# Sums of a graph attention stage with the gathered rows as stationary operand, and one load moved behind its loop

## The chip, the cores and the metric

The kernel runs on one core of one Trainium2 chip. The metric is the device time of one execution in microseconds (us); the median of three runs counts. A core has five engines that run side by side and meet through semaphores: TensorE (PE; its weight loads are PEld), VectorE (DVE), ScalarE (ACT), GpSimd (POOL) and SyncE (SP), which issues transfers. PSUM, the memory that TensorE writes, has 8 banks. An instruction that waits for a semaphore holds everything behind it on its engine.

## The reference

Four graph layers stand behind each other over 3125 nodes with 128 features and 103125 edges sorted by destination. Each adds its result to `x`. The third is the graph attention layer (GAT) with 2 heads:

```python
xl = (h @ Wl + bl).reshape(n, H, D)        # H = 2, D = 128
xr = (h @ Wr + br).reshape(n, H, D)
e = leaky_relu(xl[src] + xr[dst], 0.2)
alpha = einsum('ehd,hd->eh', e, att)
alpha = segment_softmax(alpha, dst, n)
out = segment_sum(xl[src] * alpha[..., None], dst, n).mean(axis=1)
return residual + out + h @ res_W + bias
```

The first layer is a graph convolution, the second an additive attention with 4 heads of 32 channels (same frame of a kernel stage as the third, with one bank more for each step), the fourth an interaction layer.

## The kernel before

The edges are cut into 202 tiles of 512 (4 sub-tiles of 128). The destinations of a tile lie in a window of 20 nodes. `attend` is called twice: for the second layer and, with `gat` true, for the third, in the span from about 2060 to 3360 us. What follows is the third layer's.

Each engine runs `over_tiles`: in step s it does its list of pieces, each for the tile s minus the piece's lag, and the order of the list is the order on the engine. The steps of a ring of 8 tiles make one loop body.

- POOL gathers for a tile the rows of its 512 source nodes (1 KB each) by four indirect DMAs (line 897) into one of 8 slots `rows(t)`. Before that it waits until `sums_ready` says that the tile 8 before has been summed.
- SP loads, for two tiles at once, the windows and the local places of the edges (lines 1457, 1462).
- PE in step s: `scores` of tile s-3 (lines 2101, 2106), `features` of s-1 (turns the gathered rows, line 2088, and adds the window's rows, line 2092), `turn_sums` of s-6 (line 2152), `turn_top` of s-4 (line 2128), `turn` of s-4 (the weights, line 2119), `sums` of s-5 (line 2140).
- ACT: `raise_scores` of s-3 (the exponential, line 2178), `activate` of s-1 (line 2170), `copy_sums` of s-5 (line 2184).
- DVE: `tops` of s-3 (lines 2228, 2230, 2235), `onehots` of s (line 1477), `keep_sums` of s-6 (line 2260), `leaky` of s-1 (line 2221), `best_of_nodes` of s-4 (lines 2253, 2256), `edge_weights` of s-4 (line 2246).

The sums of a tile: the stationary operand is the weights of one sub-tile and one head, 128 edges x 32 cells, the moving operand the gathered rows, 128 edges x 128 features. The result, 64 cells x 128 features for both heads, lies in bank 6. ACT copies it to `tile_rows`, PE turns it to features x cells in bank 7, DVE copies 20 of 32 cells of each head to `partial`. A product of float32 is two instructions in the records, so the 8 products of a tile are 16 records.

In `sum_counted`, a stage of the first convolution (from 452 to 600 us), the counts of one group of 24 tiles are loaded in three parts while the counts of the last tile are made again in a loop of `k.rebuild` rounds; `k.rebuild` is a number that the kernel computes, 1 for these inputs. PE waits for each part with a count that is made of it (line 1420).

## Time and profile before

| | |
|---|---|
| median of 3 runs | 4912.31 us (4910.18 to 4916.3) |
| span of the profiled execution | 4898.1 us |
| PE busy, share of the span | 3999.0 us, 82% |
| PEld | 2260.3 us, 46% |
| DVE | 2847.4 us, 58% |
| ACT | 1737.4 us, 35% |
| POOL | 2828.1 us, 58% |
| line 897, gathers of both attention stages, 1616 | about 947 ns each |
| line 2140, sums of the third layer, 3232 records | 202 x 16 |
| line 2184, copies, 202 | 252 / 258 / 262 ns (lowest, median, highest) |
| line 2152, turns, 202 | 217 / 243 / 338 ns |
| line 2260, DVE's copies, 202 | 176 / 198 / 201 ns |

The runs' times are some 14 us over the span of the records, which leaves out start and end. How to read the rows below: a row of a timeline has start, length, engine, line, operation, out<-in, shapes and in brackets the engine's idle time before it with what ended it (records of one kind are merged, xN); a row of groups has busy time, mean ns, idle time before and who ended it; a row of stretches has the length, then busy time and records of PE, PEld, DVE, ACT and POOL, PE's granted clock (1.00 is full), the share of the DMA engines and GB/s; a row of waits has the total, the number and the longest. Starts of TensorE's records can be trusted more than their ends. "issue" is waiting for nothing that the records show. Releasers are inferred: the latest event is named, which may not be the cause.

### The profile page before, as it was taken

What the parts mean: (1) busy time and instruction counts of PE and PEld (TensorE: products, weight loads), DVE (VectorE), ACT (ScalarE), POOL (GpSimd) and SP (SyncE); (2) the same over time, 40 slices, a digit from 0 to 9 for tenths busy, and PEclk for the clock granted to TensorE, in tenths of its full rate; (3) what the DMA queues carried; (4) which work ended last, traced back from release to release, by engine and by line L of the source; (5) the groups of instructions that cost most, each with busy time, mean ns of one, the idle gap of its engine ahead of it and who ended that gap; (6) DMA issues with size and microseconds to landing.
All of it is one profiled execution on the core that took longest, in us unless ns stands there. A gap on an engine that the chain in (4) does not pass through costs nothing. (4 is left out here: it accounts for less than half of the span.)

```text
span 4898.1 us, 89702 instructions
## 1 busy us (share of the span) xinstructions
PE 3999.0 (82%) x22566; PEld 2260.3 (46%) x22566; DVE 2847.4 (58%) x8457; ACT 1737.4 (35%) x4474; POOL 2828.1 (58%) x3060
## 2 busy tenths in 40 slices
PE   3997927788887877488888888885399999999987
PEld 1344414445544544344444444442256655556652
DVE  7994032333333334555555555556678888888868
ACT  3773023344344334333333333331322222222227
POOL 0122356666666663555555555554368888888862
PEclk8998957776777777688988888886699999999999
DMA  2333422222222221333333333330056666666650
GB/s 80 91 87 103 147 71 57 57 56 57 57 56 57 56 57 27 113 98 96 97 97 96 96 97 96 97 96 18 21 97 104 105 105 104 104 105 104 104 110 13
DMA packets 377425, 402.41 MB, mean 82 GB/s; under 512 B 86457, under 2 KB 322502, under 8 KB 377030
## 3 DMA queue, kind: packets, MB, share of 16 engines
q0 software_dynamic: 151904, 198.72, 21.0%
q1 hardware_dynamic: 225382, 202.21, 14.4%
q8 instruction: 43, 0.70, 0.1%
q14 instruction: 96, 0.79, 0.1%
HBM read 312.91 MB, written 87.78 MB: 82 GB/s over the span
## 5 line engine op out<-in xcount | busy, mean ns | idle before, releaser
L897 POOL DMA_INDIRECT gathered<-table,sources x952 | 903.6, 949 | 600.6 <-issue 259.9
L1709 POOL DMA_INDIRECT sums<-gathered,idx x606 | 988.7, 1632 | 217.8 <-issue 166.4
L1571 PE MATMUL bank<-wide 128*128 128x512 bf16 x3636 | 851.5, 379 | 0.0
L2228 DVE TENSOR_REDUCE neg_raw<-bank 80x1 f32<-80x512 f32 (+1 forms) x404 | 276.6, 685 | 725.9 <-remote 252.1
L897 POOL DMA_INDIRECT wide<-table,sources x464 | 438.7, 946 | 275.1 <-issue 125.7
L1571 PEld LDWEIGHTS bank<-wide 128*128 128x128 bf16 x3636 | 347.7, 98 | 364.1 <-issue 1.7
L2178 ACT ACTIVATE msg<-bank,neg_top 80x512 f32<-80x512 f32 (+1 forms) x404 | 275.7, 682 | 643.1 <-DVE neg_top L2230 353.6
L1222 POOL TENSOR_TENSOR acc<-acc,msg 128x20 f32 x404 | 108.3, 268 | 411.2 <-issue 244.6
L2221 DVE TENSOR_TENSOR zact<-zact,bank 128x512 f32<-128x512 f32 x404 | 259.5, 683 | 123.1 <-ACT zact L2170 72.9
L2106 PE MATMUL bank<-zact,att_cells 128*32 128x512 f32 x808 | 289.4, 732 | 37.9 <-issue 36.2
L2088 PEld LDWEIGHTS bank<-ident,gathered 128*128 128x128 f32 x1360 | 191.8, 165 | 258.0 <-issue 232.2
L2109 PE MATMUL bank<-zact,att_cells 128*80 128x512 f32 x404 | 301.6, 838 | 6.6 <-issue 6.6
L2246 DVE COPY edge_rows<-bank 128x320 f32<-128x320 f32 (+1 forms) x404 | 183.2, 453 | 203.5 <-remote 132.7
L2144 PE MATMUL bank<-edge_rows,gathered 128*128 128x80 f32 x1088 | 193.9, 337 | 92.5 <-DVE edge_rows L2246 81.9
L2088 PE MATMUL bank<-ident,gathered 128*128 128x128 f32 x1360 | 237.4, 317 | 35.4 <-issue 26.4
L2119 PE MATMUL bank<-ident,msg 80*128 80x80 f32 (+1 forms) x1616 | 215.5, 262 | 61.5 <-issue 33.9
L897 POOL DMA_INDIRECT h_nm<-table,sources x200 | 189.4, 947 | 130.5 <-DMA wide<-table,sources 69.3
L2190 ACT COPY partial<-bank 32x20 f32 (+1 forms) x808 | 132.6, 164 | 357.5 <-remote 239.5
L1169 DVE TENSOR_SCALAR gathered<-iota_c,partial 128x500 f16<-128x500 f16 x808 | 257.6, 339 | 1.7 <-issue 1.3
L2170 ACT ACTIVATE zact<-bank 128x512 f32<-128x512 f32 x404 | 216.8, 588 | 98.1 <-DMA window<-parts 81.2
L1178 PE MATMUL bank<-gathered,zact 128*128 128x500 f16 x812 | 209.3, 381 | 49.4 <-ACT zact L1285 28.1
L1622 ACT COPY gathered<-bank 128x437 f32<-128x437 f32 x202 | 106.1, 525 | 337.0 <-PE bank L1597 249.7
(406 smaller groups left out, 7603.9 us busy)
## 6 DMA issues: line engine op xcount, KB each, us to landing
zact<-in_src_flat SPq DMA_DIRECT2D x202, 192.0 KB
edge_rows<-in_attr_rows SPq DMA_DIRECT2D x202, 128.0 KB
dst_pair<-local_rows SPq DMA_DIRECT2D x177, 128.0 KB
gathered<-table,sources POOLq DMA_INDIRECT x952
dst_pair<-local_rows SPq DMA_DIRECT2D x202, 64.0 KB
counts<-wide SPq DMA_DIRECT2D x4, 3000.0 KB
counts<-fm_ab SPq DMA_DIRECT2D x4, 3000.0 KB
fm_ab<-counts SPq DMA_DIRECT2D x4, 3000.0 KB, 11.0
```

The costliest lines, as they stand in the source:

```text
L897: pool.indirect_dma_start(out=g[:, j, :], out_offset=None, in_=table, in_offset=bass.IndirectOffsetOnAxis(ap=mine, axis=0)).then_inc(rows_ ...
L1169: hot = dve.tensor_scalar(k.cell_hot[slot][:, j, :], k.iota_c[:, :], own, None, ALU.is_equal)
L1571: pe.matmul(k.bank[b][:, :], k.split[t.two][:, c, :], k.source_hot[t.two][:, b * CHUNK:(b + 1) * CHUNK], start=first, stop=c == PARTS - 1, ...
L1709: pool.indirect_dma_start(out=k.sums[j], out_offset=bass.IndirectOffsetOnAxis(ap=k.idx[t.slot][:, j:j + 1], axis=0), in_=out_rows(t)[:, j, ...
L2088: pe.matmul(z_bank(t, h)[:, j * P:(j + 1) * P], g[:, j, h * F:(h + 1) * F], k.ident[:, :], is_transpose=True, start=(j == 0), stop=False, ...
L2106: mm = pe.matmul(score_bank(t)[own_cells(h), :], a.att[h][:, own_cells(h)], k.zact[t.two][:, h, :], start=False, stop=True, skip_group_che ...
L2109: mm = pe.matmul(score_bank(t), a.att[0][:, :], k.zact[t.two][:, 0, :], start=False, stop=True)
L2119: mm = pe.transpose(weight_bank(t)[:, j * cells:(j + 1) * cells], raised(t)[:, j * P:(j + 1) * P], k.ident[lanes(t), lanes(t)])
L2170: act.mul(k.zact[t.two][:, h, :], z_bank(t, h)[:, :], 0.2).then_inc(slope_ready, 1)
L2178: act.activation(raised(t), score_bank(t), ACT.Exp, bias=k.neg_top[lanes(t), bass.ds(t.t, 1)], accum_out=k.weight_sum[lanes(t), bass.ds(t. ...
L2221: m = dve.tensor_tensor(za, za, z_bank(t, h)[:, :], ALU.max)
L2228: dve.tensor_reduce(raw, score_bank(t), AX.X, ALU.max, negate=True).then_inc(top_found, 1)
```

## The change

In the third layer the operands of the sums change places: the gathered rows of a sub-tile and a head (128 x 128) are stationary, and the weights (128 edges x 32 cells) move. The result is features x cells at once, 128 x 64 in bank 7. ACT's `copy_sums` and PE's `turn_sums` go, with their semaphores; DVE's `keep_sums` reads the sums themselves and waits for `sums_ready`. PE's `sums` of a tile now wait until DVE has kept those of the tile before, for the bank is one. The second layer's sums are as they were.

In `sum_counted` two parts of three are loaded in the loop, and the third once behind it, before SP's count that lets PE begin; the waits of PE are for constants.

```diff
+            second_there, rounds_done = st.sem("second_there"), st.sem("rounds_done")
...
-                    for landed in begun:
+                    for landed in begun[0:2]:
                         sp.sem_inc(landed, 16)
+
+                    def load_third(i):
+                        lo, hi = thirds[i]
+                        sp.dma_start(k.counts[0][:, lo:hi, :], k.all_counts[lo:hi, :, :].rearrange(
+                            "t p c -> p t c")).then_inc(begun[i], 16)
                     with sp.Fori(0, k.rebuild) as n:
-                        for (lo, hi), landed in zip(thirds, begun):
-                            sp.wait_ge(landed, n * 16 + 16)
-                            sp.dma_start(k.counts[0][:, lo:hi, :], k.all_counts[lo:hi, :, :].rearrange(
-                                "t p c -> p t c")).then_inc(landed, 16)
+                        for i in range(2):
+                            sp.wait_ge(begun[i], n * 16 + 16)
+                            load_third(i)
...
                         sp.sem_inc(free, 1)
+                        sp.wait_ge(begun[1], n * 16 + 32)
+                        sp.sem_inc(rounds_done, 1)
+                    sp.sem_inc(second_there, 1)
+                    load_third(2)
...
                         cell_counts(k, pe, 0, k.bank[0]).then_inc(counted, 1)
+                        pe.wait_ge(begun[0], n * 16 + 32)
...
-                            if first(now):
-                                pe.wait_ge(begun[i], k.rebuild * 16 + 16)
+                            if first(now) and i == 1:
+                                pe.wait_ge(second_there, 1)
+                            if first(now) and i == 2:
+                                pe.wait_ge(begun[2], 16)
...
-        return k.bank[6][0:cells, 0:F] if gat else k.bank[6 + t.two][:, 0:cells]
-
-    def turned_bank(t):
-        return k.bank[7][:, 0:cells]
+        return k.bank[7 if gat else 6 + t.two][:, 0:cells]
...
-                    wait_count(pe, copied if gat else kept, t.t if gat else t.t - 1)
+                    wait_count(pe, kept, t.t if gat else t.t - 1)
...
-                        for j in range(SUB):
-                            for h in range(heads):
-                                mm = pe.matmul(sum_bank(t)[own_cells(h), :], weights(t)[:, j, own_cells(h)],
-                                               g[:, j, h * F:(h + 1) * F], start=(j == 0), stop=(j == SUB - 1))
+                        for h in range(heads):
+                            for j in range(SUB):
+                                mm = pe.matmul(sum_bank(t)[:, own_cells(h)], g[:, j, h * F:(h + 1) * F],
+                                               weights(t)[:, j, own_cells(h)], start=(h == 0 and j == 0),
+                                               stop=(h == heads - 1 and j == SUB - 1), skip_group_check=True)
...
-                def turn_sums(t):
-                    pe.wait_ge(copied, t.t + 1)
-                    wait_count(pe, kept, t.t)
-                    pe.sem_inc(turns_begun, 1)
-                    pe.transpose(turned_bank(t), k.tile_rows[t.two][:, :],
-                                 k.ident[0:cells, 0:cells]).then_inc(sums_turned, 1)
                 if gat:
-                    over_tiles(pe, k.tiles, [(3, scores), (1, features), (6, turn_sums), (4, turn_top), (4, turn),
+                    over_tiles(pe, k.tiles, [(3, scores), (1, features), (4, turn_top), (4, turn),
                                              (5, sums)], ring=ring)
...
-                def copy_sums(t):
-                    act.wait_ge(sums_ready, t.t + 1)
-                    wait_count(act, sums_turned, t.t - 1)
-                    act.copy(k.tile_rows[t.two][:, :], sum_bank(t)).then_inc(copied, 1)
...
-                    over_tiles(act, k.tiles, [(3, raise_scores), (1, activate), (5, copy_sums)], ring=ring)
+                    over_tiles(act, k.tiles, [(3, raise_scores), (1, activate)], ring=ring)
...
                 def keep_sums(t):
-                    dve.wait_ge(sums_turned, t.t + 1)
+                    dve.wait_ge(sums_ready, t.t + 1)
                     dve.tensor_copy(a.partial[:, :, bass.ds(t.t, 1), :].rearrange("p z t n -> p z (t n)"),
-                                    turned_bank(t).rearrange(
+                                    sum_bank(t).rearrange(
                                         "p (z c) -> p z c", z=heads)[:, :, 0:WIN]).then_inc(kept, 1)
```

On TensorE, one step of the third layer's loop reads like this before (a row's shape is the result's; a float32 product counts once here and is two records in the trace):

```order
L2092 MATMUL bank<-onehot_t,window 128x512 x2
L2152 MATMUL bank<-ident,tile_rows 128x64
L2128 MATMUL bank<-top_cells,own 2x20
L2119 MATMUL bank<-ident,msg 128x64 x4
L2140 MATMUL bank<-gathered,edge_rows 32x128 x8
L2101 MATMUL bank<-h_nm,far 64x512
```

and like this with the change (the lines are those of the changed kernel, 8 higher here):

```order
L2100 MATMUL bank<-onehot_t,window 128x512 x2
L2136 MATMUL bank<-top_cells,own 2x20
L2127 MATMUL bank<-ident,msg 128x64 x4
L2148 MATMUL bank<-edge_rows,gathered 128x32 x8
L2109 MATMUL bank<-h_nm,far 64x512
```

The turn of the sums is gone, and the sums stand where they stood, with the operands in the other roles. On VectorE the order stays: the copy out of the bank (`partial<-bank`, line 2258 of the changed kernel) stands behind the score maximum, its two followers and the one-hot of its step, and PE's sums of the same step now wait for it:

```order
L2226 TENSOR_REDUCE neg_raw<-bank 64x1
L2228 ISA
L2228 TENSOR_SCALAR neg_top<-neg_raw 64x1
L2233 TENSOR_SCALAR top_cells<-place,neg_top 64x20
L1489 TENSOR_SCALAR h_nm<-dst_pair,iota_w,always 128x512
L2258 REGISTER_ALU
L2258 COPY partial<-bank 128x2x20
```

On SyncE, in the counts stage, three loads stood in the loop ahead of the store of the last tile's counts:

```order
L1375 DMA wide<-counts 128x8x500 x3
L1377 REGISTER_ALU
L1378 ISA
L1378 DMA counts<-fm_ab 128x500
L1372 REGISTER_ALU
L1372 COMPARE_AND_BRANCH
L1390 DMA fm_ab<-counts 128x24x500
```

With the change the third stands behind the loop, ahead of the next group's load:

```order
L1376 DMA wide<-counts 128x8x500 x2
L1382 REGISTER_ALU
L1383 ISA
L1383 DMA counts<-fm_ab 128x500
L1387 REGISTER_ALU
L1378 REGISTER_ALU
L1378 COMPARE_AND_BRANCH
L1376 DMA wide<-counts 128x8x500
L1399 DMA fm_ab<-counts 128x24x500
```

The third load has moved past the store and its landing.

## Rows read from the trace of the kernel before

**Rows 1.** Groups of instructions by shape, 2400 to 3200 us.

```profile
L897 POOL DMA_INDIRECT gathered<-table,sources x249 | 235.4, 945 | 166.4 <-DMA wide<-table,sources 97.0 <-issue 59.5 <-PE bank L2140 9.9
...
L2228 DVE TENSOR_REDUCE neg_raw<-bank 64x1 f32<-64x512 f32 x124 | 85.1, 687 | 180.4 <-DMA dst_pair<-local_rows 153.4 <-PE bank L2106 21.2 <-issue 5.0
```

**Rows 2.** Busy time by stretches: the third layer's stage, the second's.

```profile
2200.00:2700.00 500.00, 424.65 (x2957) 221.66 (x2957) 282.29 (x775) 157.85 (x386) 294.69 (x312) 0.88 0.34 97
900.00:1300.00 400.00, 334.30 (x1406) 201.95 (x1405) 132.09 (x427) 166.40 (x504) 250.64 (x264) 0.72 0.22 56
```

**Rows 3.** Timeline of all engines, one tile's period, 2711 to 2719 us.

```profile
2711.19 0.26 ACT L2184 COPY tile_rows<-bank 64x128 f32<-64x128 f32 x1 [1.42 <-DMA wide<-table,sources]
...
2711.94 0.95 POOL L897 DMA_INDIRECT gathered<-table,sources  x1 [1.91 <-DMA wide<-table,sources]
...
2712.56 1.07 PE L2140 MATMUL bank<-gathered,edge_rows 128*32 128x128 f32 x16
2712.66 0.68 ACT L2178 ACTIVATE msg<-bank,neg_top 64x512 f32<-64x512 f32 x1 [1.21 <-PE bank L2119]
...
2713.36 0.20 DVE L2260 COPY partial<-bank 128x40 f32 x1
...
2715.70 0.94 POOL L897 DMA_INDIRECT gathered<-table,sources  x1 [0.30 <-issue]
...
2715.90 0.60 PE L2092 MATMUL bank<-onehot_t,window 60*128 60x512 bf16 x2
2717.73 0.68 DVE L2228 TENSOR_REDUCE neg_raw<-bank 64x1 f32<-64x512 f32 x1 [1.45 <-DMA dst_pair<-local_rows]
2717.74 0.26 ACT L2184 COPY tile_rows<-bank 64x128 f32<-64x128 f32 x1 [3.20 <-DMA wide<-table,sources]
...
2718.14 0.29 PE L2152 MATMUL bank<-ident,tile_rows 64*128 64x64 f32 x1 [1.64 <-ACT tile_rows L2184]
...
2718.41 0.94 POOL L897 DMA_INDIRECT gathered<-table,sources  x1 [1.77 <-DMA wide<-table,sources]
```

**Rows 4.** Waits, 2400 to 3200 us.

```profile
ACT tile_rows L2184 <- DMA wide<-table,sources: 264.4, 92, 5.8
DVE neg_raw L2228 <- DMA dst_pair<-local_rows: 153.4, 67, 4.8
...
PE bank L2152 <- ACT tile_rows L2184: 70.5, 59, 4.2
```

**Rows 5.** Timeline of TensorE, a step at full clock without waits.

```profile
2739.07 0.40 PE L2101 MATMUL bank<-onehot_t,far 64*64 64x512 bf16 x1
...
2741.85 0.22 PE L2152 MATMUL bank<-ident,tile_rows 64*128 64x64 f32 x1
...
2742.13 0.46 PE L2119 MATMUL bank<-ident,msg 64*128 64x64 f32 x4
2742.52 1.07 PE L2140 MATMUL bank<-gathered,edge_rows 128*32 128x128 f32 x16
2743.51 0.40 PE L2101 MATMUL bank<-h_nm,far 64*64 64x512 bf16 x1
```

**Rows 6.** Timeline of TensorE in the second layer: full-width float32 loads.

```profile
1312.15 1.06 PE L2144 MATMUL bank<-edge_rows,gathered 128*128 128x80 f32 x8
1313.14 0.41 PE L2101 MATMUL bank<-zact,far 64*80 64x512 bf16 x1
```

**Rows 7.** Timeline of TensorE: the sums at the half clock.

```profile
2719.18 1.92 PE L2140 MATMUL bank<-wide,edge_rows 128*32 128x128 f32 x16
```

**Rows 8.** Timeline of all engines, start of the sums of counts.

```profile
465.17 0.45 PE L1195 MATMUL bank<-wide,h_nm 128*128 128x160 f16 x2 [6.74 <-SPq L1387]
```

**Rows 9.** The next groups' loads of counts, line 1390.

```profile
L1390 SPq DMA_DIRECT2D wide<-counts x4: 372/376/393, 483.0 to 575.7; - x4
```

**Rows 10.** DMA issues, 440 to 500 us: size and median time to landing.

```profile
wide<-counts SPq DMA_DIRECT2D x3, 1000.0 KB, 7.7
```

**Rows 11.** Groups of instructions by shape, second layer, 900 to 1800 us.

```profile
L2228 DVE TENSOR_REDUCE neg_raw<-bank 80x1 f32<-80x512 f32 x148 | 101.0, 683 | 304.3 <-remote 177.7 <-PE bank L2109 81.0 <-issue 45.6
```

More of the change, by code:

```diff
@@ L2049, in attend @@
         sums_ready, kept = st.sem("sums_ready"), st.sem("kept")
-        copied, sums_turned = st.sem("copied"), st.sem("sums_turned")
         cells_ready, top_turned, top_kept, best = (st.sem("cells_ready"), st.sem("top_turned"),
```

## The prediction

> **What bounds the kernel now.** I first read the groups of instructions and the busy time of the stage that the change touches, for its pace and its limits; then its waits; then one tile's timeline. The attention stage of the third layer (202 tiles, from about 2060 to 3360 us) is some 27% of the span. In 800 us of its middle 124 tiles pass (L2228 runs once a tile) [rows 1], so a tile takes 6.45 us and the stage 202 x 6.45 = 1303 us. No engine fills this: TensorE is busy 85% at a granted clock of 0.88, POOL 59%, VectorE 56%, ScalarE 32% [rows 2].
>
> POOL does more than its busy share says. It issues four gathers a tile, 0.945 us each, one every 1.25 us [rows 1, 3]; four in a row are 3 x 1.25 + 0.95 = 4.70 us, and endless ones would give 5.0 us a tile. The rest is a gap between two tiles: 2715.70 + 0.94 = 2716.64 to 2718.41, 1.77 us (0.30 would be the usual one). POOL waits there for `sums_ready`, since the sums of a tile free the slot of the next gather.
>
> The strange thing is when `sums_ready` comes. The 16 sum records of L2140 end at 2713.63, and the array goes on with L2101, L2106, L2088 and L2092 until 2716.50. But all that wait for TensorE's results resume together at 2717.7: ScalarE's copy L2184 (it waits for the sums) at 2717.74, VectorE's L2228 (for the scores) at 2717.73, POOL at 2718.41 [rows 3]. The step before is alike: the copy at 2711.19, POOL at 2711.94. So a result that the records have ended at 2713.6 is seen 4 us later, about 1 us after the last gather of the burst has ended. The views put this to "DMA" as the latest event: 264 us of ScalarE's and 153 us of VectorE's waits in 800 us [rows 4]. Of the 166.4 us that POOL idles before its 249 gathers of one name, 97.0 are put to DMA, 59.5 are the usual issue gaps, and only 9.9 are put to L2140 itself [rows 1]. I read it so: while POOL issues a burst, TensorE's signals are held, and a tile costs burst plus release plus restart, 4.70 + about 1.05 + 0.75 = 6.5 us. The cause of the hold the trace doesn't show.
>
> **The change part by part, in the attention stage.**
> *Copy and turn removed.* ScalarE loses L2184, 0.26 us a tile; it is not the limit, worth 0. TensorE loses L2152: in a tight step it and L2128 take 2742.13 - 2741.85 = 0.28 us of the array [rows 5], half of it 0.14. It also loses the wait before it (70.5 us in 59 cases of 124, 0.57 us a tile [rows 4]), but that wait is for a release that comes from the burst, so what follows is not earlier by it.
> *The sums turned round.* Before, 16 records load 32 columns each, and two heads run side by side: L2140 takes 2743.51 - 2742.52 = 0.99 us [rows 5]. After, 16 records load 128 columns and stream 32. The nearest rows are the second layer's sums, the same load of 128 x 128 f32: 8 records in 1313.14 - 1312.15 = 0.99 us [rows 6], 0.124 us each. 16 make 1.98 us, +0.99. The lowest bound is the pace of the four L2119 in the same stage, (2742.52 - 2742.13) / 4 = 0.098, which gives 1.56 us, +0.57; a gain is excluded, since a record takes 0.99 / 16 = 0.062 us now, less than either. I take +0.9, nearer to the second layer's form. A tight step is now 2743.51 - 2739.07 = 4.44 us [rows 5]; after, 4.44 - 0.14 + 0.9 = 5.2 us (4.87 to 5.29).
>
> The trace has 0.124 us for a 128-column load of 80 streamed columns, and 0.062 us a record for the 32-column loads. The Trainium skill (TensorE: Matmul & The Clock Gate, section LDWEIGHTS) says that a load's time goes with the columns loaded, P / 1.2 ns, 107 ns for 128 whatever is streamed; this would make the sums 1.71 us and the step about 5.0. It also says (TensorEngine Tiling (Array Packing), section When to Use Tiling) that with a free dimension of 64 or less one should swap the operands and tile the columns, which is what the kernel does before and the change undoes. By that rule the change makes TensorE slower, and the rows agree.
>
> *A new wait.* `sum_bank` is one bank and VectorE empties it itself, so TensorE's sums of tile s-5 wait for VectorE's keep_sums of s-6. That stands behind the score maximum, its two followers and the one-hot in VectorE's step: the release at 2711.2 (ScalarE's copy), L2260 from 2713.36 to 2713.56 [rows 3], thus 2.3 us after the release. Before, the sums began 2712.56, 1.4 us after it. Now they begin at 2.3, end at 2.3 + 1.9 = 4.2; behind them are queued scores (1.3), features (1.5) and the two turns (0.5), to 7.5 us, 1.0 us into the next period of 6.5. Who waits? POOL needs the sums by its next release at 6.5: 2.3 us of room. VectorE needs the scores (5.5) at 6.5: 1.0 of room. ScalarE's activation needs the features (7.0 = 0.5 into the next period), but it stands behind the exponential, which starts 1.5 after the release (2712.66): room again. So at the full clock all is hidden, and the period stays with POOL's burst: 0 us a tile.
>
> *At the half clock* the step is not covered so well: the 16 records of L2140 last 1.92 instead of 1.07 us [rows 5, 7], and a whole step at it is up to 2 x 5.2 = 10.4 against 2 x 4.44 = 8.9 us, +1.5. The mean of 0.88 says that a quarter of the time is at 1.2 GHz (0.24 x 1300 = 312 us, 30 to 35 steps). It falls after idle stretches of TensorE (that of 1.64 us before 2718.14, behind which the slow L2140 stands [rows 3, 7]); the new step keeps TensorE busy 0.8 us longer, so there should be fewer. I take +0.1 us of each 1.5, as the ring of 8 slots and the 1 us of room a tile take up the rest: 33 x 0.1 = 3 us.
>
> *Head and tail of the stage:* the last copy and turn go (0.26 + 0.24), the longer sums come (0.9), about +0.4 us.
>
> **The counts.** The last third of the first group's load is now issued once, behind the loop. Before, TensorE starts its sums at 465.17, when SyncE has passed `stored` [rows 8]. Now SyncE issues the third before it lets TensorE go (the increment of `loaded[0]` is behind it): an issue takes 0.37 us on L1390 [rows 9], and I take +0.5 with what stands around it, 1.5 at most. It lands about 7.7 us later [rows 10], near 474; TensorE comes to it after two thirds of the group. The next load but one, L1390 at 483.0 [rows 9], is released by the group's end, so the group lasts 17.8 us and the third is needed at 477.4. Hidden by 3 us. The next group's load of 3000 KB stands behind these 1000 KB and may come some us later than now; nothing waits for it before 483. A wait put where none was costs 0.
>
> **Sum:** 4898.1 + 3 + 0.4 + 0.5 = 4902 us of span. The median is 14.2 us over that span (4912.3), which lies outside the records and stays: 4916.2 us.
>
> **The rivals.**
> *Slower: TensorE becomes the bound.* Its step of 5.2 us at a clock of 0.88 is 5.9 us, against 6.45: only 8% of room. If every half-clock step costs its full 1.5 us: 33 x 1.5 = 50 us, 4966. If the clock fell to the second layer's 0.72 [rows 2], 5.2 / 0.72 = 7.2 us a tile, +0.77 x 202 = 156 us, 5070. It decides from the point where the step over the clock exceeds 6.45, a clock of 0.81. For it: the second layer has just this form of sums, and the lower clock. Against: the clock falls here behind idle stretches, and TensorE will have shorter ones.
> *Faster: the hold comes with the column-tiled sums.* In the step shown it begins at L2140, while the turn just ahead of it (L2119) is seen at once: ScalarE's L2178 goes on at 2712.66 [rows 3]. If full-width sums are seen when they end, at 4.2 us, POOL would not wait: 5.2 us a tile by TensorE, -1.2 x 202 = -240 us, 4670. If it only loosens to the pace of the second layer (148 tiles in 900 us [rows 11], 6.08 us), -0.37 x 202 = -75 us, 4840. Against: the second layer's sums are full-width already, and VectorE waits 177.7 us there for something that is put to no instruction [rows 11].
> *The change does nothing that lasts:* that is my forecast.
>
> **How the numbers follow.** A measurement of this kernel can tell about 0.2%, 10 us. Chances: hidden (4903 to 4922) 0.38; slower, 4922 to 4990, 0.25, and over 4990, 0.08; faster, 4840 to 4903, 0.20, and under 4840, 0.09. The range 4840 to 4990 leaves 0.17 out; the likeliest case alone is 4903 to 4922. Both signs are open, so: faster 0.29, same 0.38, slower 0.33.
>
> **What would show it.** Right: tiles still 6.45 us apart, POOL's gap still 1.8 us, the new L2148 16 records in 1.6 to 2.0 us, started by VectorE's L2258, ScalarE waiting before its exponential instead of its copy. Wrong: POOL's gaps near 0.3 us (the hold was the column tiling's), or POOL's waits put to L2148 in dozens and a clock under 0.85 (TensorE bounds). In the counts, a wait of TensorE at 477 us would show the third late.

## The result: 2% slower

| | before | changed |
|---|---|---|
| median | 4911.25 us (4 runs, 4898.11 to 4916.3) | 5009.3 us (4 runs, 5008.49 to 5011.22) |
| profiled execution, span | 4898.1 us | 5009.5 us |
| third layer, first to last of 202 tiles | 1278.0 us, 6.36 us a tile | 1372.8 us, 6.83 us a tile |
| TensorE busy, granted clock, 2200 to 2700 us | 85%, 0.88 | 100%, 0.75 |

The ratio is 1.020, 95% interval 1.019 to 1.022. The prediction was 4916 us with a range of 4840 to 4990: wrong, 93 us too low and outside its range. The two profiled executions differ by 111.4 us. Of these 94.8 lie in the attention stage of the third layer; it starts 6.9 us later (2075.2 instead of 2068.3), and 9.7 us come behind it. The last two amounts lie in code that the change does not touch, but for the counts, which became faster (below); repetitions of the kernel before differ among themselves by 18 us.

### The profile page after: what moved, and what is told of

Read it like the earlier page. It is cut to its first block and busy times, and to the rows that moved or that the text cites. A ratio compares the mean times of both kernels' runs of the same rounds, so it can differ in the third digit from the quotient of the medians.

```text
span 5009.5 us, 88649 instructions
## 1 busy us (share of the span) xinstructions
PE 4265.8 (85%) x22364; PEld 2490.1 (50%) x22364; DVE 2855.1 (57%) x8457; ACT 1700.7 (34%) x4272; POOL 2897.4 (58%) x3060
## 5 line engine op out<-in xcount | busy, mean ns | idle before, releaser
L2226 DVE TENSOR_REDUCE neg_raw<-bank 80x1 f32<-80x512 f32 (+1 forms) x404 | 277.1, 686 | 849.9 <-PE bank L2114 416.6
L2114 PE MATMUL bank<-zact,att_cells 128*32 128x512 f32 x808 | 376.5, 1031 | 15.8 <-issue 15.8
L1222 POOL TENSOR_TENSOR acc<-acc,msg 128x20 f32 x404 | 172.8, 428 | 350.0 <-issue 188.4
L2096 PEld LDWEIGHTS bank<-ident,gathered 128*128 128x128 f32 x1360 | 215.6, 183 | 307.2 <-issue 286.2
L2096 PE MATMUL bank<-ident,gathered 128*128 128x128 f32 x1360 | 258.6, 339 | 28.0 <-DMA window<-parts 16.2
L1169 DVE TENSOR_SCALAR gathered<-iota_c,partial 128x500 f16<-128x500 f16 x808 | 277.2, 373 | 7.7 <-PE bank L1178 5.9
L2153 PEld LDWEIGHTS bank<-edge_rows,gathered 128*128 128x128 f32 x1088 | 172.1, 241 | 113.1 <-DVE edge_rows L2244 75.7
```

The source lines that it names most:

```text
L1169: hot = dve.tensor_scalar(k.cell_hot[slot][:, j, :], k.iota_c[:, :], own, None, ALU.is_equal)
L2096: pe.matmul(z_bank(t, h)[:, j * P:(j + 1) * P], g[:, j, h * F:(h + 1) * F], k.ident[:, :], is_transpose=True, start=(j == 0), stop=False, ...
L2114: mm = pe.matmul(score_bank(t)[own_cells(h), :], a.att[h][:, own_cells(h)], k.zact[t.two][:, h, :], start=False, stop=True, skip_group_che ...
L2153: mm = pe.matmul(sum_bank(t), g[:, j, :], weights(t)[:, j, :], start=(j == 0), stop=(j == SUB - 1))
L2226: dve.tensor_reduce(raw, score_bank(t), AX.X, ALU.max, negate=True).then_inc(top_found, 1)
```

## The profile after

Busy time by stretches of the changed kernel; the columns are those of [rows 2]: stretch, length, busy time of PE, PEld, DVE, ACT and POOL, TensorE's granted clock, DMA share, GB/s. The first line is the whole stage, the second answers to the first line of [rows 2], the last is the second layer.

```profile
2060.00:3470.00 1410.00, 1382.55 (x7441) 813.56 (x7442) 744.02 (x2041) 374.58 (x808) 749.03 (x809) 0.74 0.30 87
2200.00:2700.00 500.00, 498.85 (x2718) 291.78 (x2716) 269.50 (x732) 136.54 (x294) 277.75 (x293) 0.75 0.32 91
...
900.00:1300.00 400.00, 325.17 (x1391) 195.63 (x1391) 131.88 (x427) 165.06 (x501) 250.55 (x264) 0.74 0.21 56
```

TensorE has no idle time left, 498.85 of 500 us, and at the same time its clock is lower: 0.75 where [rows 2] have 0.88. The second layer is as before.

Groups and waits of the changed kernel, 2400 to 3200 us (busy time and mean of one, idle time ahead and what ended it; then engine, waiting line, releaser, us, times, longest). They answer to [rows 1] and [rows 4]; L2226 is the old L2228.

```profile
L897 POOL DMA_INDIRECT gathered<-table,sources x233 | 220.8, 948 | 176.2 <-PE bank L2148 121.2 <-issue 53.1 <-DMA wide<-table,sources 1.9
...
L2226 DVE TENSOR_REDUCE neg_raw<-bank 64x1 f32<-64x512 f32 x117 | 80.6, 689 | 242.6 <-PE bank L2114 240.4 <-issue 2.2
```

```profile
ACT msg L2181 <- DVE neg_top L2228: 329.1, 68, 5.6
...
DVE neg_raw L2226 <- PE bank L2114: 240.4, 116, 2.8
...
POOL gathered L897 <- PE bank L2148: 121.2, 58, 4.1
```

117 tiles pass in 800 us where it was 124. "DMA" as the releaser has all but gone, 1.9 us where [rows 1] have 97.0: POOL now waits for the sums' own records (L2148), VectorE for the scores' (L2114). The engines wait for TensorE, and it is late because it is busy.

One period of TensorE in the changed kernel, then POOL's gathers around it (start, length, engine, line, operation, count, in brackets the idle time ahead):

```profile
2739.14 0.20 PE L2136 MATMUL bank<-top_cells,own 64*2 64x20 f32 x2
...
2739.27 0.46 PE L2127 MATMUL bank<-ident,msg 64*128 64x64 f32 x4
...
2739.66 1.97 PE L2148 MATMUL bank<-edge_rows,h_nm 128*128 128x32 f32 x16
...
2741.57 0.63 PE L2109 MATMUL bank<-onehot_t,far 64*64 64x512 bf16 x1
...
2742.13 1.92 PE L2114 MATMUL bank<-zact,att_cells 128*32 128x512 f32 x4
...
2743.98 1.53 PE L2096 MATMUL bank<-ident,wide 128*128 128x128 f32 x8
...
2745.45 0.60 PE L2100 MATMUL bank<-onehot_t,window 60*128 60x512 bf16 x2
```

```profile
2739.33 0.95 POOL L897 DMA_INDIRECT h_nm<-table,sources  x1 [0.30 <-issue]
2742.42 0.95 POOL L897 DMA_INDIRECT h_nm<-table,sources  x1 [2.14 <-PE bank L2148]
```

The 16 records of the sums take 2741.57 - 2739.66 = 1.91 us. Directly behind them the clock is at its lower level, 1.2 GHz: one bf16 record takes 0.63 instead of 0.40 us, the four of L2114 1.92 instead of 1.05. During L2096 it is back at 2.4 GHz, stays there to the end of the sums, and falls again. Taken in short stretches, the granted clock is 1.00 from 2738.2 to 2741.4 us and 0.50 from 2741.6 to 2744.8, and so on with each tile: about half of the time at either level. The next tile's L2148 begins at 2746.50, 6.84 us after this one, and many tiles in a row repeat this to one or two hundredths of a microsecond. Where the clock stays up for a step, the step is shorter:

```profile
2700.75 0.40 PE L2109 MATMUL bank<-onehot_t,far 64*64 64x512 bf16 x1
2701.08 1.05 PE L2114 MATMUL bank<-zact,att_cells 128*32 128x512 f32 x4
...
2704.17 1.96 PE L2148 MATMUL bank<-edge_rows,gathered 128*128 128x32 f32 x16
2706.05 0.40 PE L2109 MATMUL bank<-onehot_t,far 64*64 64x512 bf16 x1
```

That is 2706.05 - 2700.75 = 5.30 us, of which the sums are 1.88 and nothing is idle. The other 1.54 us of the 6.84 are the lower clock.

## The experiments

The labels' first letters are groups. The kernels of a group ran on one chip, beside the kernel before on the same chip, and the chips turned out to be of two kinds. (Each was used in one group only, so it is not shown that the chip makes the difference and not its state at the time.) On one kind before takes 4907 to 4935 us, as in the result; on the other 4381 to 4388 us. The same unchanged code of the second layer takes 6.1 to 6.2 us a tile on the first and 5.01 to 5.04 on the second. The traces tell why. On the first kind what TensorE has finished becomes visible late, as described with [rows 3]; on the second the waiting engines go on within tenths of a microsecond. I call them the late and the prompt chips. Only ratios within one group are compared.

| kernel | chip | median, us | before there | ratio (95%) | third layer, us a tile | clock in it |
|---|---|---|---|---|---|---|
| f1_counts | late | 4903.85 | 4907.42 | 0.999 (0.998 to 1.000) | 6.38 | 0.88 |
| f2_grouped | late | 4905.97 | 4907.42 | 1.000 (0.999 to 1.001) | 6.39 | 0.93 |
| f3_bank7 | late | 4962.72 | 4907.42 | 1.012 (1.010 to 1.014) | 6.60 | 0.86 |
| f4_half | late | 4903.73 | 4907.42 | 1.000 (0.998 to 1.002) | 6.35 | 0.80 |
| h1_after (the change) | late | 5016.48 | 4935.08 | 1.016 (1.014 to 1.018) | 6.86 | 0.75 |
| h2_wide | late | 5029.93 | 4935.08 | 1.020 (1.017 to 1.022) | 6.79 | 0.83 |
| h3_counts | late | 4933.93 | 4935.08 | 1.000 (0.999 to 1.001) | 6.45 | 0.88 |
| h4_early | late | 4936.66 | 4935.08 | 1.000 (0.999 to 1.001) | 6.43 | 0.82 |
| j1_counts | late | 4936.44 | 4933.26 | 1.000 (0.999 to 1.001) | 6.46 | 0.86 |
| j2_keepfirst | late | 4993.14 | 4933.26 | 1.012 (1.010 to 1.013) | 6.69 | 0.87 |
| i2_after (the change) | prompt | 4739.68 | 4387.97 | 1.080 (1.079 to 1.082) | 6.76 | 0.76 |
| i3_wide | prompt | 4490.06 | 4387.97 | 1.024 (1.022 to 1.026) | 5.50 | 0.99 |
| i1_keepfirst | prompt | 4451.05 | 4387.97 | 1.014 (1.013 to 1.016) | 5.35 | 1.00 |
| i4_pause | prompt | 4737.79 | 4387.97 | 1.080 (1.078 to 1.081) | 6.77 | 0.90 |
| g1_wide | prompt | 4493.26 | 4381.49 | 1.024 (1.022 to 1.027) | 5.55 | 0.98 |
| g2_split | prompt | 5730.28 | 4381.49 | 1.308 (1.306 to 1.310) | 11.65 | 0.50 |
| g3_pause | prompt | 4740.19 | 4381.49 | 1.082 (1.080 to 1.084) | 6.78 | 0.89 |
| g4_pausewide | prompt | 4754.16 | 4381.49 | 1.084 (1.081 to 1.086) | 6.79 | 0.89 |

The microseconds a tile are the time from the first to the last start of VectorE's reduction of the scores, over 201. The clock is that of 800 us in the middle of the stage, for g2_split of 500 us.

### Which part of the change costs

f1_counts has the change's `sum_counted` and the old `attend`.

> Only the part of the change in the counts: the register wait is mended, the sums stay as before (column-tiled, copied and turned). Both theories expect the slowdown to be that of the sums, so this kernel stays within 0.2% of before, with the counts part 2 to 3 us shorter (9.6 instead of 12.1 us from first load to first sum), and the readers of TensorE's results in the third layer again 3 to 4 us late from the start of the gathers on. If instead the slowdown of 98 us came with the counts, this kernel would be at 5009 us.

The time is that of before, and it was so twice more (h3_counts, j1_counts). The three medians differ from before's by -3.6, -1.2 and +3.2 us, all within the noise. The counts are worth nothing that can be measured in the kernel's time; their stretch did become shorter. SyncE's issues of the kernel before, then of f1_counts, and TensorE's first sum in it:

```profile
453.07 2.60 SPq L1375 DMA_DIRECT2D wide<-counts  x3
459.32 0.37 SPq L1378 DMA_DIRECT2D counts<-fm_ab  x1
```

```profile
453.17 1.02 SPq L1376 DMA_DIRECT2D wide<-counts  x2
459.46 0.37 SPq L1383 DMA_DIRECT2D counts<-fm_ab  x1
462.07 0.37 SPq L1376 DMA_DIRECT2D wide<-counts  x1
```

```profile
462.55 0.45 PE L1195 MATMUL bank<-wide,h_nm 128*128 128x160 f16 x2 [3.96 <-SPq L1396]
```

From the first load to the first sum 462.55 - 453.17 = 9.38 us, where before had 465.17 [rows 8] - 453.07 = 12.10. The store (`counts<-fm_ab`) is what TensorE's start hangs on; with two loads ahead of it instead of three it is done 2.6 us after its issue (462.07), before it took until about 465.1. The transfers' own account agrees: from issue to landing the store takes 2.2 us in f1_counts and 5.5 us before.

So the loss is that of the sums: what the counts add to it is under the noise.

### Is it TensorE's work?

f4_half leaves half of the products of the sums out (and with them half of the result):

```diff
-                            for j in range(SUB):
+                            for j in range(SUB // 2):
```

> The changed kernel with half of the products of its sums left out (8 records a tile instead of 16), so that a part of the result is not computed. If TensorE's time is what now bounds the third layer, each tile gets at least 0.95 us shorter: 4820 us or less, down to 4640 us where GpSimd at 5.0 us a tile takes over. If waits between the engines set the 6.84 us a tile, the time stays at 5009 us.

With 8 records less a tile, 0.95 us, all of the 98 us come back: 4903.73 beside 4907.42. But no more than that, so neither of the two times expected came (4820 us or less, or 5009). The tile takes 6.35 us as before, not 5.0. And the signals are late again, with the very form of products under which they looked prompt:

```profile
2656.15 0.96 POOL L897 DMA_INDIRECT gathered<-table,sources  x1 [0.30 <-issue]
2656.16 0.65 PE L2100 MATMUL bank<-h_nm 60*128 60x512 bf16 x2
...
2657.27 1.08 PE L2148 MATMUL bank<-edge_rows,gathered 128*128 128x32 f32 x8
2657.41 0.95 POOL L897 DMA_INDIRECT gathered<-table,sources  x1 [0.30 <-issue]
...
2660.05 1.09 ACT L2173 ACTIVATE zact<-bank 128x512 f32<-128x512 f32 x2 [3.67 <-DMA window<-parts]
...
2660.99 0.95 POOL L897 DMA_INDIRECT gathered<-table,sources  x1 [2.63 <-DMA wide<-table,sources]
```

L2100 ends at 2656.81 and L2148 at 2658.28. ScalarE, which waits for L2100, goes on only at 2660.05, and POOL, which waits for L2148, at 2660.99. POOL's last gather ended at 2658.36; the release comes 1.69 us behind it (1.1 in [rows 3]). So, as I read it, there are two limits that lie close together on this chip: the old one (a burst of gathers plus the late release, 6.4 us a tile) and TensorE's step, 6.84 us with its clock down. The change went from the first to the second.

### Were the late signals a matter of the column-tiled sums?

Both kernels keep the old sums with the counts of the change. f2_grouped puts all products of head 0 ahead of those of head 1, so that neighbours no longer lie on different columns of the array. f3_bank7 puts the sums into bank 7, turns them there too, and waits for VectorE as the change does:

```diff
 # f2_grouped
-                        for j in range(SUB):
-                            for h in range(heads):
+                        for h in range(heads):
+                            for j in range(SUB):
 # f3_bank7
-        return k.bank[6][0:cells, 0:F] if gat else k.bank[6 + t.two][:, 0:cells]
+        return k.bank[7][0:cells, 0:F] if gat else k.bank[6 + t.two][:, 0:cells]
-        return k.bank[7][:, 0:cells]
+        return k.bank[7][:, F:F + cells]
-                    wait_count(pe, copied if gat else kept, t.t if gat else t.t - 1)
+                    wait_count(pe, kept, t.t if gat else t.t - 1)
```

> The counts of the change, and the sums column-tiled as before, but with all products of one head before those of the other, so that no two neighbours lie on different columns of the array. Theory A (late signals come from products of two column groups that run interleaved): signals are prompt, the 16 products take 1.6 to 2.0 us, and the time is 4700 to 4850 us. Theory B (column tiling or the small stationary operand as such makes the signals late): still 3 to 4 us late, 4910 us and, if the sums take longer without their neighbour, up to 0.5 us a tile more. Theory C (the bank or the waits around the sums): still late, 4910 us.

> The counts of the change, and the column-tiled sums of before, but in bank 7 and with the wait that the changed kernel has in front of its sums. Theory C (what the change took away is a matter of the bank or of where the sums wait): signals are prompt and the time is 4700 to 4850 us. Theories A and B (the form of the products): signals still 3 to 4 us late, the new wait is hidden, 4900 to 4925 us.

In both the signals stay late (ScalarE's copy of the sums waits 223.0 us in 71 cases for "DMA" in 800 us of f3_bank7, 267.1 us in 91 cases in f1_counts), so theories A and C fall, and f4_half took B away. The form of the sums does not make the signals late. Grouped, the 16 records take 1.53 instead of 1.07 us (without a neighbour on the other columns), and this costs nothing that can be measured. Turned round they take 1.97 by the same rows, so about half of what the change adds to the sums comes already with the loss of the side-by-side products.

f3_bank7 missed its expectation in a way that matters: 59 us more than f1_counts. A wait of this kind, which the prediction called hidden, is not. TensorE's wait in 800 us of f3_bank7:

```profile
PE bank L2152 <- DVE partial L2272: 132.0, 75, 6.1
```

The wait for VectorE's copy holds TensorE 132 us in 75 cases. In the changed kernel the wait at this place is 3.1 us, since TensorE there comes to it late anyway. The two are not quite the same wait: in f3_bank7 VectorE's copy must itself wait for ScalarE's copy and TensorE's turn, which the changed kernel no longer has, so 59 us is more than the changed kernel's wait need cost. The keepfirst kernels below price that one.

### What brings the clock down?

g1_wide, h2_wide and i3_wide are one kernel: the changed one, with each product streaming the weights of both heads, 64 columns instead of 32. The half that is of the other head is never read.

```diff
-        return k.bank[7 if gat else 6 + t.two][:, 0:cells]
+        return k.bank[7][:, 0:3 * cells] if gat else k.bank[6 + t.two][:, 0:cells]
...
-                                mm = pe.matmul(sum_bank(t)[:, own_cells(h)], g[:, j, h * F:(h + 1) * F],
-                                               weights(t)[:, j, own_cells(h)], start=(h == 0 and j == 0),
+                                mm = pe.matmul(sum_bank(t)[:, h * cells:(h + 1) * cells], g[:, j, h * F:(h + 1) * F],
+                                               weights(t)[:, j, :], start=(h == 0 and j == 0),
```

> The changed kernel, but each product of the sums streams the weights of both heads (64 columns instead of 32) and the half that is of the other head is not read. At full clock a product is bound by its load of 128 columns (118 ns a record), so the sums still take about 1.9 us. Theory P (the clock falls because so few columns are streamed in the stretch of the sums): the granted clock in the third layer rises from 0.74 to 0.85 or more, TensorE's step falls under 6.45 us a tile, and the limit of before takes over again (GpSimd's burst of four gathers, signals of TensorE held until about 1 us behind it): 6.4 to 6.5 us a tile, 4890 to 4925 us. Theory Q (the clock falls because TensorE has no idle time): clock stays near 0.74 and the time at 4990 to 5030 us, up to 5080 us if the wider products take longer.

The clock is that of theory P, 0.98. Neither theory's time can be judged, because g1_wide ran on a prompt chip, where the changed kernel had not run. i2_after and i3_wide put both on one chip, again a prompt one.

> The changed kernel as the anchor of this call. Where signals are late (before at 4905 to 4935 us): 5009 to 5016 us. Where they are prompt (before at 4381 us): by theory P (few streamed columns let the clock fall, whatever the signals do) 6.84 us a tile here too and 4760 to 4800 us, over 200 us above the wide kernel's 4493 us; by theory R (the clock falls only together with late signals) 4480 to 4500 us like the wide one.

> The wide kernel (64 streamed columns) beside it. Where signals are late: 5015 to 5040 us, clock 0.83 in the third layer. Where prompt: 4493 us, clock 0.98, 5.5 us a tile.

Stretches of 800 us of i2_after, then of i3_wide, then of i1_keepfirst (i3_wide with another order on VectorE, described below):

```profile
2000.00:2800.00 800.00, 799.58 (x4379) 471.03 (x4378) 434.78 (x1184) 219.07 (x473) 447.40 (x473) 0.76 0.32 92
```

```profile
2000.00:2800.00 800.00, 791.13 (x5409) 513.57 (x5410) 533.76 (x1461) 263.07 (x584) 552.47 (x586) 0.99 0.39 113
```

```profile
2000.00:2800.00 800.00, 800.00 (x5564) 523.61 (x5565) 544.19 (x1505) 269.51 (x601) 568.20 (x602) 1.00 0.40 117
```

TensorE idles 0.4, 8.9 and 0.0 us in them. With 32 streamed columns its clock is 0.76, with 64 it is 0.99 and 1.00, and i3_wide is 250 us faster than i2_after although it streams twice the columns. The third row leaves no room for theory Q: busy all of the 800 us, TensorE keeps its full clock. A step of the wide one on the prompt chip:

```profile
2403.62 0.40 PE L2109 MATMUL bank<-h_nm,far 64*64 64x512 bf16 x1
2403.95 1.05 PE L2114 MATMUL bank<-zact,att_cells 128*32 128x512 f32 x4
2404.94 1.09 PE L2096 MATMUL bank<-ident,wide 128*128 128x128 f32 x8
...
2407.26 1.97 PE L2148 MATMUL bank<-edge_rows,gathered 128*128 128x64 f32 x16 [0.18 <-DVE partial L2258]
2409.16 0.40 PE L2109 MATMUL bank<-onehot_t,far 64*64 64x512 bf16 x1
```

The wide sums take 2409.16 - 2407.26 = 1.90 us, as the narrow ones: at this size the weight load sets the pace, and the doubled columns are free. So the clock does not fall here because TensorE is idle, and not because it is busy. It falls behind the 1.9 us in which TensorE loads weights and streams 32 columns a product, and stays up behind the same 1.9 us with 64 (theory P); that the number of streamed columns makes the difference is shown by this one edit, how the chip weighs them is not. The Trainium skill (TensorE: Matmul & The Clock Gate, section HAM oscillation) gives as its rule to leave no long idle gaps on TensorE; i2_after has none, 0.42 us of idle time in 800 us, and runs at 0.76.

g2_split was to tell a long stretch of such products from the mean of the period: the products of head 0 moved to behind the scores.

```diff
-                    over_tiles(pe, k.tiles, [(3, scores), (1, features), (4, turn_top), (4, turn),
-                                             (5, sums)], ring=ring)
+                    over_tiles(pe, k.tiles, [(3, scores), (5, first_sums), (1, features), (4, turn_top), (4, turn),
+                                             (5, sums)], ring=ring)
```

> The changed kernel, with the products of head 0 moved to behind the scores, so that the 16 products of a tile stand in two stretches of 8 with the tile's transposes of the gathered rows between them; same work. Theory P1 (a long stretch of products with few columns makes the clock fall): clock up to 0.85 or more, 4890 to 4930 us. Theory P2 (what counts is the work of the whole period, not where it stands): clock about 0.74, 5000 to 5020 us.

Neither came: 5730 us. The first products now wait right behind the scores until VectorE has emptied the bank of the tile before, and that copy stands in VectorE's step behind the reduction of those scores:

```profile
PE bank L2144 <- DVE partial L2267: 145.5, 68, 2.3
```

That is 2.1 us in each of 68 tiles of 800 us, and the clock is at 0.50 through the whole stage, with TensorE busy 82%. It says that the lower level can last for 2.3 ms; since a wait was added with the split, it does not decide between P1 and P2.

### And on the late chip?

> The changed kernel once more, on the same chip as the other three of this call, as their anchor. On a chip where TensorE's signals come late while GpSimd issues (before at 4907 us): 5009 us again, granted clock 0.74 in the third layer and 6.84 us a tile. On a chip where they come promptly (before at 4381 us, as in the call with the wide and the paused kernels): slower than before as well, by more than the 112 us of the wide kernel if the clock falls here too (6.84 us a tile, 4760 to 4800 us), by 80 to 112 us if it does not.

> The changed kernel with 64 instead of 32 streamed columns in each product of its sums, again. Where signals are late: theory P (few streamed columns let the clock fall) has the clock back at 0.85 or more, and TensorE no longer bounds the tile, so that the 6.4 to 6.5 us of before return, 4890 to 4930 us. Theory Q (being busy without a break lets the clock fall) has it at 0.74 and 5000 us or more. Where signals are prompt: 4493 us again, 5.5 us a tile, and by theory P over 200 us less than the changed kernel, by theory Q the same as it.

> The sums of before with the counts of the change, as the picture of the kernel before on this chip: within 0.2% of before on either. Where before takes 4907 us the signals of TensorE come 3 us late from the start of the gathers on; where it takes 4381 us they are prompt, a tile of the third layer takes about 5.0 us, and GpSimd's burst of four gathers (4.7 us) is what bounds it.

Here the clock rises as well, 0.75 to 0.83, and it gives nothing: 5029.93 beside 5016.48. So theory P has nearly its clock and misses its time by 100 us. Where the clock is up, TensorE's step of 5.3 us is under the old limit, and POOL's gathers show the old picture. h2_wide:

```profile
2705.79 1.39 PE L2148 MATMUL bank<-edge_rows,gathered 128*128 128x64 f32 x11
...
2707.11 0.40 PE L2109 MATMUL bank<-onehot_t,far 64*64 64x512 bf16 x1
...
2707.53 0.95 POOL L897 DMA_INDIRECT gathered<-table,sources  x1 [0.30 <-issue]
...
2710.34 0.94 POOL L897 DMA_INDIRECT gathered<-table,sources  x1 [1.87 <-DMA wide<-table,sources]
```

The sums end at 2707.11, inside the burst; POOL resumes at 2710.34, 1.86 us after its last gather's end, and the wait is put to DMA again. In the changed kernel the sums end at 2741.57, and POOL's last gather had ended at 2740.28: TensorE is so late that nothing is left to hold. I take this to be why the signals looked prompt there.

Why, then, does h2_wide lose 95 us? Half of POOL's bursts in it start 6.3 to 6.7 us apart, but in the whole stage 18 pairs, the stage's first left aside, are 8 to 9.7 us apart. The kernel before, f1_counts and h3_counts have no such pair. In all 18 TensorE is at its lower clock for half of the time or more. Here are three rows of TensorE and one of POOL in such a period, and then its stretch in the columns of [rows 2]:

```profile
2158.40 0.63 PE L2109 MATMUL bank<-onehot_t,far 64*64 64x512 bf16 x1
2164.45 3.67 PE L2148 MATMUL bank<-edge_rows,gathered 128*128 128x64 f32 x16
2168.06 0.63 PE L2109 MATMUL bank<-onehot_t,far 64*64 64x512 bf16 x1
2168.92 0.95 POOL L897 DMA_INDIRECT gathered<-table,sources  x1 [4.95 <-PE bank L2148]
```

```profile
2159.26:2168.92 9.66, 9.66 (x39) 6.08 (x37) 4.58 (x14) 1.86 (x4) 3.79 (x5) 0.50 0.24 73
```

A step of TensorE at the lower clock takes 2168.06 - 2158.40 = 9.66 us without a pause, 3.61 of them the sums, and POOL waits for it. On a late chip the turned sums therefore cost by the steps that fall into the lower clock, even where the mean clock is most of the way back.

j2_keepfirst and i1_keepfirst take the wait for the bank out of the wide kernel, by putting VectorE's copy at the head of its step:

```diff
-                    over_tiles(dve, k.tiles, [(3, tops), (0, onehots), (6, keep_sums), (1, leaky),
+                    over_tiles(dve, k.tiles, [(6, keep_sums), (3, tops), (0, onehots), (1, leaky),
```

> The wide kernel, with VectorE's copy of the sums put at the head of its step, ahead of the reductions and the one-hot rows, so that bank 7 is free sooner. If the wait for the bank is what is left where the clock stays up (21 to 48 us of TensorE's idle time in 800 us of the wide kernel), 20 to 50 us less than the wide kernel; if TensorE's step and the late signals bound it, the same within 0.3%.

> The wide kernel with VectorE's copy of the sums at the head of its step, again. Where signals are prompt: 4451 us (a TensorE step of 5.3 us against GpSimd's 5.0 us a tile), 60 us above before. Where signals are late: if the wait for bank 7 is what keeps the wide kernel at 5030 us, 4950 to 5000 us; if the late signals do, 5010 us or more.

39 us less than the wide kernel on the prompt chip (4451.05 for 4490.06). On the late ones the loss against before went from 94.9 to 59.9 us, 35 us less. It is the best kernel with the whole of the sums turned round, and still slower than before on both: on the prompt chip its tiles are 5.32 us apart, each a full TensorE step without a break. Before is 63 us faster there, which over 202 tiles is 0.31 us a tile less, an estimate of 5.0 us: the pace of POOL's four gathers at one every 1.25 us. The 60 us that remain on a late chip can be followed in the traces of j2_keepfirst and j1_counts. I sort the distances between the starts of POOL's bursts, from the tenth tile on, by the mean clock granted in them. At 0.95 or more they are alike, 6.29 us (110 of 192) and 6.33 us (95). At 0.60 or less they are 8.04 us (27) and 6.53 us (17). 27 x (8.04 - 6.29) = 47 us less 17 x (6.53 - 6.33) = 3 us makes an estimate of 44 us, and the two profiled executions differ by 42.8. What remains is thus the steps at the lower clock again. The mean clock of the stage doesn't show it, 0.87 in j2_keepfirst and 0.86 in j1_counts. In j1_counts the time at the lower clock comes in 62 stretches, 6 of them over 8 us, in j2_keepfirst in 33, 17 of them over 8 us, up to 24, so that whole steps fall into it. With the wait for the bank in place, in h2_wide, the distances at 0.95 or more are 6.51 us (82) against 6.32 in h3_counts (96): 0.19 us a tile, 38 us in 202, is what this wait costs at the full clock.

h4_early moves the old sums 0.6 us forward, ahead of the turns of the weights:

```diff
-                    over_tiles(pe, k.tiles, [(3, scores), (1, features), (6, turn_sums), (4, turn_top), (4, turn),
-                                             (5, sums)], ring=ring)
+                    over_tiles(pe, k.tiles, [(3, scores), (1, features), (6, turn_sums), (5, sums),
+                                             (4, turn_top), (4, turn)], ring=ring)
```

> As h3_counts, with the turn of the old sums and the sums put ahead of the two turns of the weights on TensorE, which brings them 0.6 us nearer to the start of GpSimd's burst. If signals are held only from about 1.5 us behind the burst's start on, more of the sums' signals get out before that, GpSimd finds its buffer free at the burst's end, and a tile takes less than 6.45 us: 4700 to 4880 us. If they are held whatever the place: 4905 us. Where signals are prompt: within 0.2% of h3_counts.

Nothing: 4936.66 beside 4935.08 before and 4933.93 for h3_counts. Moving the sums by 0.6 us does not matter.

### Does a gap in POOL's issuing end the hold?

```diff
+        if pause and j == SUB // 2:
+            pool.wait_ge(rows_loaded[t.slot][j - 1], (t.rounds + 1) * 16)
```

> The sums as before (column-tiled) with the counts of the change, and GpSimd waiting in the third layer, between the second and the third gather of each tile, until the rows of the second have landed: about 1.1 us without issuing. If what holds TensorE's signals ends as soon as GpSimd's queue has nothing under way, the signals come in this pause, the next burst no longer waits for the end of this one, and the time stays at 4850 to 4920 us in spite of the pause. If the hold lasts until the tile's last gather, each period is 1.1 us longer: 7.5 us a tile, 5060 to 5100 us.

> The two together: the changed sums with 64 streamed columns, and GpSimd's pause between the second and the third gather. If both help, a tile takes about 5.9 us (a burst of 4.7 us and a pause of 1.1 us), and the time is 4800 to 4840 us; if the pause only lengthens the period, 7.5 us a tile and 5060 to 5100 us.

> The old sums with GpSimd waiting between the second and the third gather of each tile until the second's rows have landed (it took 1.8 us a tile where signals are prompt, 6.76 us a tile, 4740 us). Where signals are late: if they come out in the pause, the period is again the burst with its pause, 6.76 us a tile and 4960 to 5010 us; if they wait for the tile's last gather, 8.0 us a tile or more and over 5150 us.

All three fell on prompt chips, where nothing is held, so the question was not put. They show the other thing: the pause makes a tile 6.8 us, with the old sums as with the wide ones, since there POOL's issuing is the limit: 5.0 us and 1.8 us for the landing. The old sums with the pause (i4_pause, prompt chip) show what a prompt signal looks like, against [rows 3]:

```profile
2405.94 1.07 PE L2154 MATMUL bank<-gathered,edge_rows 128*32 128x128 f32 x16
...
2407.12 0.26 ACT L2198 COPY tile_rows<-bank 64x128 f32<-64x128 f32 x1 [0.58 <-PE bank L2154]
2407.24 0.95 POOL L899 DMA_INDIRECT gathered<-table,sources  x1 [2.09 <-PE bank L2154]
```

The sums end at 2407.0, ScalarE copies at 2407.12 and POOL issues at 2407.24, in place of 4 us later.

## Why the prediction was wrong, point by point

- **The size of the sums: right.** +0.9 us forecast, with bounds of 0.57 and 0.99; measured 1.88 to 1.91 against 0.99 us. The step at full clock was to be 5.2 us and is 5.30. The Trainium skill (TensorEngine Tiling (Array Packing), section When to Use Tiling) advises to swap the operands and tile the columns where 64 columns or fewer are streamed; undoing this took the sums from 0.99 to 1.9 us here, so the advice held.
- **The clock: the step that failed.** That "the clock falls here behind idle stretches, and TensorE will have shorter ones" was read off one place, the slow L2140 behind an idle stretch [rows 3, 7]. The changed kernel has next to no idle time (1.15 of 500 us) and a lower clock, 0.75 for 0.88; i1_keepfirst has none either and the full clock. The counter-example stood in the rows: the second layer, with sums of the full-width form, had 0.72 at the same share of busy time [rows 2]. The prediction cites it as a rival ("if the clock fell to the second layer's 0.72") and gives it too little. Put into the deciding condition of that rival (step over clock above 6.45 us, below a clock of 0.81), the measured step and clock give 5.30 / 0.75 = 7.1 us; measured are 6.84, so the part of the step that ran at the lower clock slowed down by somewhat less than two. Which part did is not separated.
- **The half clock's 3 us** is the term of the sum that was mis-sized. It was 33 steps of 0.1 us. In the changed kernel half of nearly every step is at the lower clock, which adds 1.54 us to 5.30; beyond what the old limit hid, that is 6.83 - 6.36 = 0.47 us a tile, 94.8 us in the stage. The 0.1 us had no row behind it: it left most of a slow step to the slots and the room. In h2_wide a whole step at the lower clock is 9.66 us (10.4 at most by the working), 3.2 over the usual period, and POOL waits for it.
- **The rival that came** is "TensorE becomes the bound". Its mechanism is shown for the changed kernel (f4_half, i3_wide). The measured 5009 us lie between its two figures, 4966 and 5070.
- **The new wait: right in the result, wrong in the reason.** It cost nothing (3.1 us in 800) because TensorE came late to it. In kernels where TensorE has room it cost 35 to 39 us (the keepfirst kernels), and a longer chain at the same place 59 us (f3_bank7). The working put the wait at one phase of one period and took the period as steady; [rows 3] are of a single tile.
- **The faster rival** seemed to come true, since late signals vanished from the stage. By my reading they vanished because TensorE fell behind; f4_half brought them back.
- **The counts: wrong sign, small.** +0.5 us forecast, -2.7 measured from the first load to the first sum, and nothing measurable in the kernel's time. The working looked at what the third load is late for, and not at what it had stood ahead of in the queue: the store on which TensorE's start depends.
- **The range** took the slow side to 4990. Even with most of the clock back the turned sums cost 95 us on a late chip (h2_wide), and 60 without the wait for the bank (j2_keepfirst). The sorted periods say which part of "so at the full clock all is hidden" held. The longer sums are hidden there (6.29 beside 6.33 us without the wait); the new wait is not (0.19 us a tile with it), so the room of 1.0 to 2.3 us that was read from one period [rows 3] is not there in all of them. The larger part of the loss is again the half clock, whose slow steps the forecast had taken for nearly free.

## What to carry to other kernels

Turning a product round so that the wide side becomes stationary made it take 1.9 instead of 0.99 us here, with 32 streamed columns as with 64; count it against TensorE's step. A product that loads much and streams little can also take the clock from the work behind it, as it did here: if such products can't be avoided, compare the stage's clock with that of a stage that has them already, and try streaming more columns in the shadow of the load. And price the step at the lower clock by itself, not at the mean: 5.3 us at the full clock were under the other limit of 6.45 us, 9.66 us at the lower one were not, and the mean of the two hides this.

## What the runs showed of the hardware that I had not expected

- With TensorE busy in 799.6 of 800 us the granted clock was 0.76 (i2_after), and doubling the streamed columns of the sums brought it to 0.99 in the same time of those products (1.9 us, i3_wide); with TensorE busy in all of 800 us it was 1.00 (i1_keepfirst). In g2_split it stayed at 0.50 for the whole stage of 2.3 ms, with TensorE busy 82%.
- Chips differ, or their states. On the chips of three groups (f, h, j) TensorE's results became visible up to 4 us late while POOL issued gathers, and the kernel before took 4907 to 4935 us; on those of two (g, i) I saw none late, and the same kernel took 4381 and 4388 us, 11% less. What holds the signals, and why only on some chips, stays open: it is not the form of the sums (f2_grouped, f4_half), not their bank or wait (f3_bank7) nor, within 0.6 us, their place (h4_early), and whether a gap in POOL's issuing ends it was never tried on such a chip.
- The same change costs 1.6 to 2.0% on a late chip and 8.0% on a prompt one, where the lower clock has no slack to hide in: 250 of the 352 us go with the clock (i2_after less i3_wide).
